# First batch's row maxima sent in two halves, hyper products and weight splits re-ordered around its attention, par_f and a raw weight loaded sooner, the scaling of h2 moved on DVE

## The reference, cut to what matters

```
x = x + alpha_a * attention(gamma*rmsnorm(x)+beta)          # 16 heads of 16, softmax over 256 keys
x = x + alpha_f * swiglu(gamma*rmsnorm(x)+beta)             # 1024 hidden, bias on the way out
x = x + ternary(down_w) @ quant(val * gelu(gate))           # 1024 hidden, rows quantised to 127 steps
Wd_b = Wd + 0.1*(h_lang @ Wdd.T + bdd)   (same for Wu_b)    # an adapter of its own for each batch
x = x + relu(x @ Wd_b.T + bd) @ Wu_b.T + bu
x = layernorm(x)*weight + bias + tanh(...), once more scaled
```

## Time and profile before

| | before |
|---|---|
| median of 3 runs | 991.65 us |
| the profiled execution's own time | 995.88 us |
| its span, first to last instruction | 993.6 us |
| PE busy in it | 949.1 us (96%) |
| mean granted clock of TensorE | 0.979 |

### The profile page before, as it was taken

One profiled execution on the slowest core, in us unless ns is written; L12 is line 12 of the kernel. 1 busy time (PEld: TensorE's weight loads), 2 busy tenths in 40 slices (PEclk: granted clock), 3 DMA queues, 4 the chain that ended last, 5 costly groups with the idle time before them and its releaser, 6 DMA issues.

```text
span 993.6 us, 21359 instructions
## 1 busy us (share of the span) xinstructions
PE 949.1 (96%) x6770; PEld 786.5 (79%) x6770; DVE 733.2 (74%) x1700; ACT 578.1 (58%) x1197; POOL 259.4 (26%) x343
## 2 busy tenths in 40 slices
PE   8777989999999999999999999999999999998997
PEld 7345659888887979888887979788888979786776
DVE  5843458787878788787877878787877878785756
ACT  3265554756656574856666574847666574746532
POOL 2162502223131322222131322222231322211220
PEclk9787999999999999999999999999999999999999
DMA  7897652040404022130404022130404021130000
GB/s 217 285 317 305 213 193 75 31 121 3 149 1 128 21 78 70 44 106 1 149 1 138 11 86 62 44 106 1 149 1 141 9 96 53 48 92 2 22 17 17
DMA packets 75776, 89.43 MB, mean 90 GB/s; under 512 B 16528, under 2 KB 62112, under 8 KB 73184
## 3 DMA queue, kind: packets, MB, share of 16 engines
q1 hardware_dynamic: 70816, 71.19, 23.4%
q0 software_dynamic: 1440, 9.18, 2.6%
q10 hardware_dynamic: 3488, 8.65, 2.4%
HBM read 63.14 MB, written 25.31 MB: 89 GB/s over the span
## 4 chain that ended last, share of the span: by engine, by line
PE 78%; DVE 8%; DMA 6%; issue 3%; ACT 3%; SPq 1%; POOL 0%; ACTq 0%; DVEq 0%; POOLq 0%
PE bank L771 17%; PE bank L835 15%; PE bank L785 8%; PE bank L730 7%; PE bank L740 6%; PE bank L712 6%; PE bank L748 3%; PE bank L852 3%; DMA hyper<-w_hyper 2%; PE bank L872 1%; PE bank L692 1%; PE bank L845 1%; PE bank L866 1%; DMA par_f<-cond_dram 1%; PE bank L650 1%
## 5 line engine op out<-in xcount | busy, mean ns | idle before, releaser
L581 POOL TENSOR_TENSOR act_lo<-act_f,act_hi 128x256 fp32r<-128x256 f32 x120 | 88.3, 736 | 372.8 <-ACT act_hi L1229 372.8
L1497 DVE TENSOR_REDUCE neg_max<-bank 128x2 f32<-128x512 f32 x256 | 162.1, 683 | 0.4 <-PE bank L712 0.4
L1176 ACT ACTIVATE probs<-bank 128x512 f32<-128x512 f32 x256 | 135.2, 602 | 23.6 <-PE bank L730 11.7
L1265 ACT ACTIVATE gelu_g<-bank,r 128x256 f32<-128x256 f32 x128 | 60.6, 474 | 91.5 <-PE bank L835 88.9
L1223 ACT ACTIVATE silu_g<-bank 128x256 f32<-128x256 f32 x128 | 49.1, 383 | 104.1 <-PE bank L771 103.8
L771 PE MATMUL bank<-h_hi,gh_hi 128*128 128x256 f32 x512 | 104.3, 286 | 5.1 <-DVE h_lo L1569 5.1
L771 PE MATMUL bank<-h_lo,gh_hi 128*128 128x256 f32 x512 | 103.7, 284 | 0.0
L771 PE MATMUL bank<-h_hi,gh_lo 128*128 128x256 f32 x512 | 103.4, 284 | 0.0
L1575 DVE TENSOR_TENSOR act_f<-bank,silu_g 128x256 f32<-128x256 f32 x128 | 53.7, 420 | 65.1 <-ACT silu_g L1223 65.1
L1229 ACT ACTIVATE act_hi<-act_f 128x256 fp32r<-128x256 f32 x128 | 53.4, 417 | 75.5 <-DVE act_f L1575 73.7
L771 PEld LDWEIGHTS bank<-h_hi,gh_hi 128*128 128x128 f32 x512 | 83.8, 191 | 14.2 <-issue 9.3
(11 more groups left out here) (232 smaller groups left out, 2091.1 us busy)
## 6 DMA issues: line engine op xcount, KB each, us to landing
q_stack<-q_dram SPq DMA_DIRECT2D x96, 128.0 KB
k_stack<-k_dram SPq DMA_DIRECT2D x90, 128.0 KB
q_dram<-probs SPq DMA_DIRECT2D x16, 512.0 KB, 2.8
k_dram<-probs SPq DMA_DIRECT2D x16, 512.0 KB, 2.8
hyper<-w_hyper POOLq DMA_DIRECT2D x8, 1024.0 KB, 10.2
hyper<-w_hyper SPq DMA_DIRECT2D x8, 1024.0 KB, 6.8
x_res<-xT SPq DMA_DIRECT2D x16, 256.0 KB, 2.8
out<-xc SPq DMA_DIRECT2D x15, 256.0 KB, 2.5
```

What stands on the lines that cost most here:

```text
L581: pool.tensor_tensor(act_lo[:, c % 3, :], act_f[:, c % 2, :], act_hi[:, c % 3, :].bitcast(F32), ALU.subtract).then_inc(g_lo.sem, 1)
L1176: act.activation(probs[:, h % SLOTS], halves(SCORE_BANKS[h]), ACT.Exp, scale=float(H / D) ** 0.5).then_inc(s_exp.sem, 1)
L1265: act.activation(gelu_g[:, n % 2, :], halves(7 - n % 2)[:, 1, :], ACT.Gelu, scale=r3[:, t:t + 1])\
L1497: dve.tensor_reduce(neg_max[:, qt, :, pair:pair + 1].rearrange("p a o -> p (a o)"), halves(n % 3), AX_X, ALU.max, negate=True).then_inc(ma ...
```

## The change

- **Maxima in halves.** For batch 0, after `max_scores` 10 PE turns the maxima of heads 0 to 7 (`half_turn(0)`, into bank 4), ACT copies them (`half_row_out`) to `first_rows`, SP sends them (`rows_half`). Heads 8 to 15 follow when all maxima are there. `scores` of head 0 wait for the first half's landing (`half_dma`), those of head 8 for the second's (`max_dma`). `neg_max` holds the pair ahead of the parity; for the other batches only the layout differs.
- **Hyper products.** 0 and 1 move from ahead of the scores to behind `attend` 0 and 1; 2 and 3 come behind `attend` 3; 4 and 5 behind the projection of v. Their evictions on ACT move along: pieces 0 and 1 between the exponentials, 4 and 5 to the end of the step; `hyper_evict(2)` goes behind `normalise(a, 1)`.
- **Weights.** `high_part(0)` runs between the two row copies, `high_part(2)` after `guess_f`; raw weight 2 is loaded after exponential 3; raw weight 3 is loaded by SP behind the stacks, no longer by ACT, which waited for the stacks' landing before it. POOL does `low_part(0)` ahead of its wait for the maxima. On DVE the copy of raw weight 1 stands between the halves of `ternary_down`.
- **par_f.** For batch 0 it is loaded in step 0, behind `load_res`, and not in step 1.
- **h2, in every step.** `scaled_f` is cut in two: `normed_f` (the product) stays behind `gated_u(0)`, the scale and shift go behind `gated_u(1)`.

```diff
@@ sync: run @@
-                    if f:
-                        if f.follows():
-                            sp.wait_ge(n3_lo.sem, n3_lo.at(f, back=1))
+                    if f and f.follows():
+                        sp.wait_ge(n3_lo.sem, n3_lo.at(f, back=1))
                         sp.dma_start(par_f[:].rearrange("p k c -> p (k c)"),
                                      cond_of(f, F_ALPHA, L1_SCALE)).then_inc(par_f_dma.sem, 16)
...
+                    if starts(a):
+                        sp.wait_ge(half_row.sem, 1)
+                        sp.wait_ge(max_mm.sem, 8)
+                        rows_half(first_rows, 0, half_dma)
...
                     if starts(a):
+                        rows_half(second_rows, 1, max_dma)
                         sp.wait_ge(cond_out.sem, 16)
                         load_res(a)
+                        sp.dma_start(par_f[:].rearrange("p k c -> p (k c)"),
+                                     cond_of(a, F_ALPHA, L1_SCALE)).then_inc(par_f_dma.sem, 16)
...
                     if starts(a):
+                        sp.dma_start(w_raw[:, 3, :], raw[3][0]).then_inc(raw_in[3].sem, 16)
                         sp.wait_ge(hyper_ev_dve.sem, by_dve(2))
@@ tensor: scores, run @@
-                    if h == 0:
+                    if h == 0 and starts(b):
+                        pe.wait_ge(half_dma.sem, 32)
+                    if h == 6 and starts(b):
+                        pe.wait_ge(max_row.sem, max_row.at(b))
+                    if h == (8 if starts(b) else 0):
                         pe.wait_ge(max_dma.sem, max_dma.at(b))
                         pe.wait_ge(max_row.sem, max_row.at(b))
...
-                        if starts(a) and c >= FC:
-                            hyper_product(c - FC)
...
-                        if starts(a) and t >= 2:
+                        if starts(a) and t < 2:
                             hyper_product(t)
...
                     if starts(a):
-                        hyper_product(4)
+                        hyper_product(2)
+                        hyper_product(3)
...
                     if starts(a):
+                        hyper_product(4)
                         hyper_product(5)
@@ scalar: run @@
-                    act.preload_act_table_set("natural_log_exp_and_others")
+                    if f:
+                        act.preload_act_table_set("natural_log_exp_and_others")
...
-                    if starts(a):
-                        hyper_out_piece(0)
-                        hyper_out_piece(1)
-                        high_part(0)
-                        act.wait_ge(max_dma.sem, max_dma.at(a))
-                        raw_load(2)
...
+                            if starts(a) and h == 3:
+                                raw_load(2)
+                            if starts(a) and h in (7, 13):
+                                hyper_out_piece(h // 8)
...
-                        act.wait_ge(stack_dma.sem, stack_dma.at(nxt, 16 * 8))
-                        raw_load(3)
+                        high_part(2)
@@ gpsimd @@
+                low_part(0)
                 pool.wait_ge(max_dma.sem, max_dma.at(Batch(0)))
-                for n in range(2, EARLY - 1):
-                    hyper_load(pool, n)
-                low_part(0)
+                hyper_load(pool, 2)
+                hyper_load(pool, 3)
                 low_part(1)
-                hyper_load(pool, EARLY - 1)
+                hyper_load(pool, 4)
+                hyper_load(pool, 5)
                 low_part(2)
@@ vector: run @@
                         if a and n == 0:
+                            normed_f(a)
+                        if a and n == 1:
                             scaled_f(a)
```

More of the change, by code:

```diff
@@ L159, in build @@
         den_x = sb("den_x", [P, T])
+        first_rows, second_rows = few_rows[0:H // 2, :].bitcast(F32R), den_raw[0:H // 2, :].bitcast(F32R)
         o_norm = sb("o_norm", [P, DC, T])
@@ L398, in load_res, with rows_half @@
                                  cond_of(b, NEG_ALPHA, F_BETA)).then_inc(x_res_dma.sem, 16)
+                def rows_half(src, half, done):
+                    at = slice(half * (NPAIR // 2), (half + 1) * (NPAIR // 2))
+                    for par in range(2):
+                        sp.dma_start(q_stack[64 * par + 63:64 * par + 64, at, :].bitcast(F32), src[par:H // 2:2, :].bitcast(F32))\
+                            .then_inc(done.sem, 16)
                 def run(a, f, g, nxt):
@@ L717, in max_turn, with half_turn @@
                     for t in range(TT):
-                        mm = pe.transpose(bank[0][0:H, t * P:(t + 1) * P], neg_max[:, t].rearrange("p a m -> p (a m)"), ident[:])
+                        mm = pe.transpose(bank[0][0:H, t * P:(t + 1) * P], neg_max[:, t].rearrange("p m a -> p (m a)"), ident[:])
                     mm.then_inc(max_t.sem, 1)
-                def scores(b, h, nxt=None):
-                    if h == 0:
+                def half_turn(half, done):
+                    pe.wait_ge(max_red.sem, 8 * (half + 1))
+                    if half == 1:
+                        pe.wait_ge(half_row.sem, 1)
+                    for t in range(TT):
+                        mm = pe.transpose(bank[4][0:H // 2, half * T + t * P:half * T + (t + 1) * P],
+                                          neg_max[:, t, half * (NPAIR // 2):(half + 1) * (NPAIR // 2)].rearrange("p m a -> p (m a)"),
+                                          ident[:])
+                    mm.then_inc(done.sem, 1)
+                def scores(b, h, nxt=None):
+                    if h == 0 and starts(b):
[3 more added lines that the diff above has]
+                    if h == (8 if starts(b) else 0):
                         pe.wait_ge(max_dma.sem, max_dma.at(b))
@@ L919, in run @@
                             if starts(a):
-                                pe.wait_ge(small_in.sem, 16 * 6)
-                            max_turn(a)
+                                half_turn(1, max_t)
+                            else:
+                                max_turn(a)
+                        if starts(a) and c == 4:
+                            pe.wait_ge(small_in.sem, 16 * 6)
+                            half_turn(0, half_t)
                         if nxt and f and c == FC:
@@ L1168, in max_row_out, with half_row_out @@
                     act.activation(max_rows, bank[0][0:H, 0:T], ACT.Copy).then_inc(max_row.sem, 1)
+                def half_row_out(half, src_done, to, done):
+                    act.wait_ge(src_done.sem, 1)
+                    act.activation(to, bank[4][0:H // 2, half * T:(half + 1) * T], ACT.Copy).then_inc(done.sem, 1)
                 def exps(b, h):
@@ L1306, in run @@
                     for c in range(FC + 1):
-                        if a and c == FC:
+                        if a and c == FC and not starts(a):
                             max_row_out(a)
+                        if starts(a) and c == FC:
+                            half_row_out(0, half_t, first_rows, half_row)
+                            high_part(0)
+                            half_row_out(1, max_t, second_rows, max_row)
                         if f and c >= 1:
@@ L1386, in run @@
                     if starts(a):
+                        hyper_out_piece(4)
                         hyper_out_piece(5)
@@ L1496, in row_max @@
                             dve.wait_ge(max_t.sem, max_t.at(b, back=1))
-                    dve.tensor_reduce(neg_max[:, qt, :, pair:pair + 1].rearrange("p a o -> p (a o)"), halves(n % 3), AX_X, ALU.max,
+                    dve.tensor_reduce(neg_max[:, qt, pair, :], halves(n % 3), AX_X, ALU.max,
                                       negate=True).then_inc(max_red.sem, 1)
@@ L1743, in run @@
                     if starts(a):
-                        ternary_down()
+                        ternary_scale()
+                        ternary_down((0, 1))
                         dve.wait_ge(raw_in[1].sem, 16)
                         dve.tensor_copy(raw[1][1], w_raw[:, 1, :]).then_inc(w_hi_dve.sem, 1)
+                        ternary_down((2, 3))
                     if nxt and f:
@@ L1758, in run @@
                         normalise(a, 0, g)
-                    if starts(a):
-                        hyper_evict(2)
                     if starts(f):
@@ L1770, in run @@
                         normalise(a, 1)
+                    if starts(a):
+                        hyper_evict(2)
+                    if a:
                         normalised(a, 1)
```

34 lines of the change are left out of this document (18 added, 16 removed).

## The result

| | before | changed |
|---|---|---|
| median, 20 runs each | 991.48 us (989.53 to 994.53) | 987.42 us (982.23 to 990.50) |
| ratio | | 0.9948, 95% interval 0.9935 to 0.9961 |
| profiled execution: own time, span | 995.88, 993.6 us | 990.35, 988.0 us |
| mean granted clock in it | 0.979 | 0.980 |

The changed kernel is 4.1 us faster by the medians and 5 by the ratio: the right side, but no more than half of the 10.5 us that I had forecast. The median lies 0.9 us above my range; by the ratio, set against the 991.65 that I started from, the time is 986.5, the range's upper edge.

The account below looks back on a forecast made before the run. PE was taken as the bound in the steady state, behind a start-up chain with waits for `par_f` and the stacks. 4.2 us from h2 plus 6.3 from the start-up gave 10.5 us, 981.2; range 977.5 to 986.5.

Parts of the forecast that it names:

- point 6: POOL's loads of pieces 6 and 7, asked for 1.5 us later; product 6 at 82.6, giving back 1.5 of 3.2 us.
- 1, h2: Up product of every step: chunk 3 no longer waits behind the scalings; 0.28 us times 15 steps, 4.2 us.
- Rival D: Up product: the wait moves to chunk 4, the h2 edit gives under 1 us; 985.4, chance 0.15.
- 2, halves: Rows of maxima: first half lands at 47.2 to 47.5, in order behind `cond_dram`; under 0.5 us, none counted.
- rival C: First rows overtake `cond_dram`: scores start at 43, later stations come some 5 us sooner; 976.2, chance 0.05.
- 3, exponentials: ACT in attention: exponentials start 2.4 us sooner, take in 2.5 us of other work, end at 61.4; zero gain.
- 4 and 5, h2 and gate of batch 0: Between attention and gate: h2 ready at 73.6, no wait for the stacks, gate at 75, 3.2 us sooner.
- 7, par_f: Step 1: no wait for `par_f`, silu 3 at 89.9, gate 5 at 94.4; 7.3 us in all with full clock.
- 8, the discount: Start-up: a stretch at half clock may remain, 1 to 2.5 us; 1.0 taken off, leaving 6.3 us.
- A: The start-up stall moves to `x_in` of batch 2, landing at 84 to 87; 984.5, chance 0.15.
- B: Stacks land at 77, `x_in` at 96.6, silu 3 at 103.3; 994.5, slower from a landing at about 94; chance 0.04.
- E: Only the h2 edit works; loads of pieces 8 to 15 take back the start-up's gain; 987.4, chance 0.06.

Follow-up runs that it names:

- h2 alone: The kernel before with only the cut of `scaled_f`; 988.14 us, ratio 0.9965.
- h2 undone: The changed kernel with `scaled_f` again right behind `normed_f`, ahead of `gated_u(1)`; 992.89 us, ratio 1.0013 to the kernel before.
- x_in ahead: The changed kernel with `x_in` and `par_a` of batch 2 sent by SP ahead of raw weight 3; 986.20 us, ratio 0.9952 to the kernel before.
- whole rows: The changed kernel with the first half of the maxima sent only just ahead of the second half; 988.01 us, ratio 0.9953 to the kernel before.
- low part behind: The changed kernel with POOL's `low_part(2)` started only when ACT has taken h2 of batch 0; 988.64 us, ratio 0.9970 to the kernel before.
- both alone: The kernel before with only the cut of `scaled_f` and `par_f` of batch 0 loaded in step 0; 983.66 us, ratio 0.9928.
- the pair above: Two ratios to the kernel before: everything in the change but h2 (h2 undone) 1.0013, and par_f alone 0.9967.
- par_f alone: The kernel before with only `par_f` of batch 0 loaded in step 0, none in step 1; 988.81 us, ratio 0.9967.
- raw 4 late: The changed kernel with raw weight 4 asked for by ACT two chunks later; 987.26 us, ratio 0.9954 to the kernel before.

## Why the prediction was half right

**The step that failed is where the start-up's gain was taken from:** "I take differences and set them against the median". The profile of before reached up at 143.89 us, h2 alone with the same code at 138.65, and the median run of before near 138.4 (the estimate above), so all of the 4.2 us by which that profile lay above the median was start-up. My 6.3 us, taken off 143.89, put up at 137.6; h2 undone has it at 137.18, x_in ahead at 137.59, and the median run of the changed kernel near 138.5. So the place was nearly met, but seen from the median run it is no gain. The second failure, piece 6, is in point 6.

*1, h2:* right. Forecast 0.28 us a step, measured 0.32 (55.63 to 55.31), 3.5 us in all by h2 alone. Rival D's wait at chunk 4 didn't come.

*2, halves:* the worth was right, nothing, but not the reason. The scores that wait for the rows began at 46.6 to 48.1 us in all seven profiles with the changed order of products 0 and 1, whether the rows were sent at 38 us or at 43. I took it that SP's transfers go in order; in three of these profiles the rows were in 1.0 to 1.3 us ahead of `cond_dram`. The Trainium skill (DMA: Bandwidth & Descriptors, Queues, rings and completion order) lets a small later transfer finish first, and these three agree; what never came is the size that rival C gave it, 4 to 5 us. And my row for it was misread: in the kernel before the scores at 47.77 stood directly behind product 1 (45.90 to 47.83), so they don't show when the rows landed.

*3, exponentials:* right within 1 us (over at 60.44 instead of 61.4).

*4 and 5, h2 and gate of batch 0:* the places of the steps were right but not their sizes. `h_hi` came at 75.45, not 73.6, since POOL's `fo_lo` runs beside the scalings; I had moved `low_part(2)` without asking what runs beside it. `h_lo` took 0.98 us instead of 0.69 there, too, and ended at 77.09. Gate came at 77.34, not 75, 0.25 us behind `h_lo`, as in before (0.26) and in h2 undone (0.25). Product 5, whose wait for its piece until 76.27 I had not costed, ended just then and so cost nothing at gate.

*6, the load that is late next:* **this term failed.** I let pieces 6 and 7 be asked for at 77.6, with the stacks in by 76, and gave piece 6 "some 5 us". It took 9.7 us from issue to landing in the changed kernel's profile, 7.2 in h2 undone, where it was asked for at 77.84, as forecast, 7.2 to 9.1 in x_in ahead, whole rows and low part behind, and 6.8 with raw weight 4 out of its way; before, it had taken 7.9. The 5.0 us were those of raw weight 3. So product 6 came at 85.04 in the best of these profiles instead of 82.6, and silu 3 at 93.20 instead of 89.9. In the changed kernel's own profile the stacks were late too, at 79.79; I had named pieces 4 and 5 beside them and taken their cost from no row, though three loads in a row stood on POOL before and the changed order has a product between each. Instead of 3.2 us gained and 1.5 given back, the rest of the change costs 2 (both alone against changed, 0.9928 to 0.9948, intervals that meet) to 4.5 us (the pair above, whose intervals don't). Which part of the rest costs this stays open: with `par_a`, `low_part(2)`, raw weight 4 or products 0 and 1 moved, one at a time, the interval of the ratio still met the changed kernel's.

*7, par_f:* the mechanism was right: 3.3 us when alone. Two things made it 7.3 in my sum. I took the gain of point 5 into it, which piece 6 eats (0.5 of 2.75 us left). And I measured it against one execution whose start-up was long: its stretch at half clock and silu 5 at 103.38, where the same code in h2 alone had a granted clock of 0.76 there, silu 5 at 102.09, and began up 5.2 us sooner. I had noted that its own time lay 4.2 us above the median, and still took its differences whole.

*8, the discount:* a stretch at half clock did remain, but the "1 to 2.5 us" behind my 1.0 come from no row. In h2 undone product 6 took 1.94 us instead of 1.06 and the 12 matmuls of `gate` behind it 2.31 instead of 1.62: 1.6 us.

*Rivals:* A's place was right, its size (984.5) wasn't: the square waited, but for `par_a`, up to 92.34, where A had a landing at 84 to 87, and only in some executions. B's landing (94 or later) didn't come. E gives the measured 987.4 by a mechanism that par_f alone refutes. From the Trainium skill's rule beside A, in the same section, that an engine drains a packet of 9 to 17 pieces from one ring before it turns, I had concluded that so few pieces cost nothing; 23.0 us for 2 KB refutes the conclusion. Whether it refutes the rule is open, since I put no price on a turn, and the pieces of the 1 MB loads beside it are 8 KB each.

## What to carry to other kernels

When a product that frees a load buffer is moved later, list every load behind that buffer and what each one will now meet: here it showed up 30 us on, in transfers that nobody touched. Where a change has cheap independent parts, time them alone before adding gains up; here two edits of a few lines were worth 7 us, and the careful re-ordering around them took some of it back. And don't take a gain out of one profile of a part that varies from execution to execution; look first how that profile stands to the median, and compare the time at which it reaches a fixed point (here the first up product) with that of another profile of the same code.

## What the runs showed of the hardware

A 2 KB parameter load took 6.2 us (both alone), 11.4, 15.0, 18.0 or 23.0 us from issue to landing, where `x_in`, issued half a microsecond earlier on the same queue, took 5.7, 11.4, 12.4, 9.7 and 13.0. So it can trail its neighbour by 10 us while megabyte loads of other queues run.

On one queue, two loads of 4 KB issued 5.7 to 6.5 us behind a store of 144 KB to DRAM landed 1.0 to 1.3 us ahead of it in three of the profiles (h2 undone, x_in ahead, raw 4 late). So this queue didn't finish its transfers in order.

The two DVE scalings of batch 0, 128x256 each, took 0.73 to 0.82 us together with POOL idle, 0.90 to 0.91 where the last 0.4 us of POOL's four subtractions of 128x512 ran beside the first of them, and 2.40 to 2.43 in the seven profiles where POOL's subtractions ran beside them throughout. The subtraction `h_lo` on DVE (128x512) took 0.98 to 0.99 us in those seven and 0.69 in the other seven.

Late in the program, the step that ends with the up product near 910 us took 55.2 to 56.0 us in nine profiles and 54.4 to 54.7 in the other five, in kernels built on the one before as in those built on the changed one. In the long ones TensorE's granted clock was 0.91 to 0.96 from 906 to 926 us, in the short ones 1.00. Here is that stretch in the changed kernel (the last three numbers are the granted clock, the DMA share and GB/s):

```profile
906.00:926.00 20.00, 16.66 (x75) 12.36 (x65) 14.29 (x39) 10.56 (x23) 4.69 (x7) 0.91 0.09 26
```

The profile of before had 1.00 there and a step of 54.72 us, where the changed kernel had 55.88, which hid another 1.2 us of the gain in the comparison of the two profiles. In the changed kernel the 0.91 is the mean over one short stretch at TensorE's lower level (1.2 GHz): 0.50 from 911 to 913 us, behind two microseconds (908 to 910) in which TensorE was busy for 0.02 us, most of it waiting for DVE's `o_norm`. x_in ahead has a pause like it and kept 1.00; why was not seen.
